# Fused block with a mixture of experts: the first eight expert tiles fixed when the kernel is written, two of them fed by one-hot products

## What is computed

```
x = x + tanh(g_ffn[1]) * ffn(layernorm(x))

logits = gelu(x @ rw1) @ rw2                 # router, E = 8
wgt, idx = top_k(softmax(logits), 2)
for e in range(E):
    Ye = gelu(x @ w1[e] + b1[e]) @ w2[e] + b2[e]
    Ce = gelu(b1[e]) @ w2[e] + b2[e]          # what an expert gives to a token that isn't its own
    for k in range(2):
        mask = idx[..., k] == e
        active = any(mask)
        out += active * wgt[..., k] * where(mask, Ye, Ce)
```

## Time and profile before

| | |
|---|---|
| time, median of 3 runs | 430.28 us (429.59 to 430.42) |
| time of the profiled execution | 430.72 us |
| its span | 428.8 us |
| mean granted TensorE clock in it | 0.898 |
| instructions | 8535 |
| busy: TensorE, VectorE, ScalarE, GpSimd | 319.6, 307.7, 262.0, 166.6 us |
| HBM read, written | 27.43 MB, 6.32 MB |

### The profile page before, as it was taken

One profiled execution on the slowest core, in us unless ns is written; L12 is line 12 of the kernel. 1 busy time (PEld: TensorE's weight loads), 2 busy tenths in 40 slices (PEclk: granted clock), 3 DMA queues, 4 the chain that ended last, 5 costly groups with the idle time before them and its releaser, 6 DMA issues.

```text
span 428.8 us, 8535 instructions
## 1 busy us (share of the span) xinstructions
PE 319.6 (75%) x2638; PEld 216.0 (50%) x2639; DVE 307.7 (72%) x739; ACT 262.0 (61%) x528; POOL 166.6 (39%) x231
## 2 busy tenths in 40 slices
PE   0065988869999968777582511578999999999981
PEld 0054337536477635354341210365777777777760
DVE  3998988863764666759676689466788788888870
ACT  1745656623576476848687598033677777777770
POOL 3041301531284260623671659200355444444422
PEclk9997799989999998979788565678999999999997
DMA  8954000140076073411313535834477777777532
GB/s 265 389 144 136 2 0 2 53 142 2 0 165 233 2 208 72 141 50 51 99 50 99 159 92 147 315 130 171 149 247 248 246 245 245 236 248 233 157 36 24
DMA packets 28097, 60.43 MB, mean 141 GB/s; under 512 B 4401, under 2 KB 19010, under 8 KB 24866
## 3 DMA queue, kind: packets, MB, share of 16 engines
q1 hardware_dynamic: 21186, 52.64, 35.6%
q0 software_dynamic: 4416, 6.13, 8.9%
q10 hardware_dynamic: 2464, 1.27, 1.2%
HBM read 27.43 MB, written 6.32 MB: 79 GB/s over the span
## 4 chain that ended last, share of the span: by engine, by line
DVE 36%; PE 32%; issue 11%; ACT 11%; DMA 4%; POOL 3%; ACTq 1%; DVEq 0%; POOLq 0%
PE bank L1202 6%; PE bank L1544 4%; PE bank L1562 4%; ACT arena L1063 4%; DVE MX L1902 4%; DVE arena L2080 2%; PE bank L1547 2%; PE bank L1163 2%; DVE X L1748 2%; ACT arena L1070 2%; DVE arena L2164 2%; DVE arena L2159 2%; PE bank L1565 2%; DVE stats L1626 2%; ACT arena L945 2%
## 5 line engine op out<-in xcount | busy, mean ns | idle before, releaser
L1063 ACT ACTIVATE arena<-arena,B1D 128x128 f32<-128x128 f32 x184 | 57.6, 392 | 14.3 <-DVE arena L2159 13.7
L1562 PE MATMUL bank<-arena 128*128 x184 | 62.3, 385 | 1.2 <-DVE arena L2164 1.2
L2159 DVE TENSOR_REDUCE arena<-bank 128x256 f32<-128x512 f32 x92 | 57.4, 683 | 4.6 <-PE bank L1547 4.6
L663 POOL TENSOR_TENSOR arena<-STG,arena 128x256 f16<-128x256 f32 x56 | 37.1, 695 | 42.4 <-ACT arena L835 42.4
L663 POOL TENSOR_TENSOR W<-STG,W 128x256 f16<-128x256 f32 x64 | 41.4, 683 | 28.3 <-ACT W L835 28.3
L1565 PE MATMUL bank<-arena 128*128 x184 | 50.7, 276 | 0.0
L734 POOL DMA_INDIRECT out_dram<-arena,SI x23 | 37.3, 1621 | 31.0 <-DMA out_dram<-arena,SI 23.7
L721 POOL DMA_INDIRECT arena<-token_rows,GI x23 | 22.8, 991 | 66.5 <-ACT WS L1057 51.3
L2164 DVE SCALAR_TENSOR_TENSOR arena<-arena 128x512 f16<-128x512 f32 x46 | 29.8, 689 | 24.8 <-ACT arena L1070 24.8
L1544 PE MATMUL bank<-arena 128*128 128x256 f16 x256 | 46.4, 281 | 1.5 <-DVE arena L2127 1.1
L1547 PE MATMUL bank<-arena 128*128 128x128 f16 x256 | 45.4, 225 | 0.0
(11 more groups left out here) (266 smaller groups left out, 708.5 us busy)
## 6 DMA issues: line engine op xcount, KB each, us to landing
STG<-in_l_w_dram SPq DMA_DIRECT2D x32, 512.0 KB, 3.6
arena<-W SPq DMA_DIRECT2D x16, 1024.0 KB, 5.0
STG<-W SPq DMA_DIRECT2D x7, 1024.0 KB
arena<-in_l_w_dram SPq DMA_DIRECT2D x2, 1280.0 KB, 12.2
X<-in_x_dram SPq DMA_DIRECT2D x2, 512.0 KB, 6.1
W<-in_ctx_t_dram ACTq DMA_DIRECT2D x2, 512.0 KB, 11.2
W<-in_ctx_dram SPq DMA_DIRECT2D x1, 1024.0 KB, 17.6
k_parts<-W SPq DMA_DIRECT2D x2, 512.0 KB, 3.3
```

Source lines behind the costliest of these rows:

```text
L663: ins = nc.gpsimd.tensor_tensor(l, src, h, ALU.subtract)
L1063: ins = nc.scalar.activation(x, x, ACT.Gelu, bias=B1D[:, e, c:c + 1], scale=1.0 / (X_SCALE * W_SCALE))
L1562: nc.tensor.matmul(bank[6 + q][:, :], GDL[:, q, 0, c * P:(c + 1) * P], W2[:, e, c].rearrange("p s d -> p (s d)"), start=(c == 0), stop=Fal ...
L2159: v.tensor_reduce(half, o, AX.X, ALU.add).then_inc(s_dadd, 1)
```

## The change

**First eight tiles.** Each expert's first 128 tokens are tile 0 to 7, in the order STATIC = 4, 5, 6, 7, 0, 1, 2, 3, which is known when the kernel is written. They need no EID, no copy of the weights (TensorE reads W1 directly), and no registers. The 15 other tiles take the experts' further tokens. A slot is now the rank within the expert plus ENDT, or plus `place` where the rank is below 128 (early, DIFF).

**Tiles 0 and 1** get their transposed rows as products of the token rows in SBUF (DHL) with one-hot matrices OH (128x1024 each) that come from the ranks (RANK1): 32 products of 128x128 for each tile. Their rows are still gathered, for the row weights alone.

**Slot map and gather.** The products for the slot map (slot_tokens) stand behind tile 0's up product, GI and SI behind tile 0's reductions. GpSimd gathers tiles 2, 3, 0, 1, 4 in this order. Rows and outputs have three buffers. All 23 tiles are written out, without loops.

**Idle shares** move behind tiles 6 to 14 on TensorE: transposes of coefficients at tiles 6 and 7, all 128 products of the idle outputs at 8, the fold at 10, the shares at 11 to 14. ScalarE writes them out (coefficients_out, group_outputs_out, idle_outputs_out, shares_out) over X. SP stores the base X ahead of the tiles (store_base). GpSimd adds the shares, 1 MB, to the output with one direct adding DMA (add_shares) between the adds of tiles 15 and 16.

**Weight blocks.** ScalarE splits blocks 28 to 31 at tiles 3, 4, 5 and 5. GpSimd subtracts for blocks 25 and 26 behind the first five gathers and for 27 to 31 behind the adds of tiles 0 to 4. VectorE's two subtractions fall away. SP's first copy of tile weights (tile 8) waits for all 32 blocks.

The diff, cut to its core:

```diff
@@ constants
+        ONE_HOT = 2
+        STATIC = [*range(E // 2, E), *range(E // 2)]
...
+        SHARES_AFTER = 15
+        def added(j):
+            return 16 * (j + 1 + (j > SHARES_AFTER))
@@ SP
+            def store_base(h):
+                sp.wait_ge(s_dhs, HT * (h + 1))
+                sp.dma_start(out[h * HT * P:(h + 1) * HT * P, :].rearrange("(t p) d -> p t d", p=P),
+                             X[:, h * HT:(h + 1) * HT, :]).then_inc(s_out, 16)
...
             sp.wait_ge(s_eid, 1)
-            sp.wait_ge(s_wlo, W1_BLOCKS)
-            sp.wait_ge(s_rows, 16 * 3)
...
+            sp.wait_ge(s_gi, 2)
+            sp.wait_ge(s_xt_ps, ONE_HOT)
+            sp.wait_ge(s_ws, ONE_HOT)
+            sp.wait_ge(s_wlo, BLOCKS)
+            for j in range(E, TILES):
+                load_tile_weights(j)
@@ GpSimd
+            def add_shares(n):
+                pool.wait_ge(s_share, T)
+                pool.wait_ge(s_sc, 16 * n)
+                pool.dma_start(out[0:N, :].rearrange("(t p) d -> p t d", p=P), X[:, :, :],
+                               accum_op=ALU.add).then_inc(s_sc, 16)
...
-            for j in range(4):
+            for j in (2, 3, 0, 1, 4):
                 gather_rows(j)
+            for i in D_BLOCKS[4:6]:
+                weights_low(i)
...
             for j in range(TILES):
-                if j + 4 < TILES:
-                    gather_rows(j + 4)
+                if j + 5 < TILES:
+                    gather_rows(j + 5)
                 add_to_out(j)
+                if j == SHARES_AFTER:
+                    add_shares(j + 1)
+                if j < BLOCKS - D_BLOCKS[6]:
+                    weights_low(D_BLOCKS[6] + j)
@@ ScalarE
+            def shares_out(t):
+                act.wait_ge(s_base, t // 2 + 1)
+                act.wait_ge(s_out, 32)
+                for i in range(2):
+                    nc.scalar.activation(X[:, t + i], bank[1][:, i * D:(i + 1) * D], ACT.Copy,
+                                         scale=tg[:, 3:4]).then_inc(s_share, 1)
+            for j in range(TILES):
...
+                tile_gelu(j)
...
+                if j >= 3:
+                    low_out(j - 1)
+                if j in (3, 4, 5):
+                    weights_split(D_BLOCKS[4 + j])
+                if j == 5:
+                    weights_split(D_BLOCKS[10])
...
+                if j in (12, 13, 14, 15):
+                    shares_out(2 * (j - 12))
@@ TensorE
+            def one_hot_rows(j):
+                pe.wait_ge(s_oh, j + 1)
+                for k in range(KC):
+                    for s in range(2):
+                        for t in range(T):
+                            mm = nc.tensor.matmul(bank[j][:, (2 * k + s) * P:(2 * k + s + 1) * P],
+                                                  DHL[:, t, s, k * P:(k + 1) * P], OH[:, j, t],
+                                                  start=t == 0, stop=t == T - 1)
+                mm.then_inc(s_xt_ps, 1)
...
+            for j in range(ONE_HOT):
+                one_hot_rows(j)
+            for j in range(TILES):
...
+                tile_up(j, e)
+                if j == 0:
+                    slot_tokens()
+                if ONE_HOT <= j + 1 < TILES:
+                    transpose_tile(j + 1)
+                if j:
+                    tile_down(j - 1, e_before)
...
+                if j == 8:
+                    idle_outputs()
+                if j == 10:
+                    fold_groups()
+                if j in (11, 12, 13, 14):
+                    idle_shares(2 * (j - 11))
@@ VectorE
+            step(v.scalar_tensor_tensor(out=RANK1[:, :, :], in0=rank[:, :, ones_hot], scalar=1.0,
+                                        in1=MSB[:, :, ones_hot], op0=ALU.add, op1=ALU.mult))
+            for j in range(ONE_HOT):
+                v.tensor_tensor(OH[:, j], iota_1[:, :].unsqueeze(1).broadcast_to([P, T, P]),
+                                RANK1[:, :, j:j + 1].broadcast_to([P, T, P]), ALU.is_equal).then_inc(s_oh, 1)
...
+            for j in range(TILES):
+                add_halves(j)
+                if j == 0:
+                    slots_out()
...
+                if j == 1:
+                    tile_experts()
+                    coefficients()
```

More of the change, by code:

```diff
@@ L418, in flamingo @@
         s_base = sem("idle_share_product")
[L419 to L420 removed]
+        s_oh = sem("first_tiles_one_hots_ready")
+        s_xrs = sem("first_tiles_rows_landed")
+        s_xr = [sem(f"tile_rows_landed{i}") for i in range(3)]
+        s_share = sem("idle_shares_in_sbuf")
         s_w1s = [sem(f"tile_weights_landed{i}") for i in range(3)]
@@ L1067, in tile_gelu @@
                     act.wait_ge(s_dg, 2 * j + hb + 1)
-                    if not first:
+                    if j >= 2:
                         act.wait_ge(s_dd, j - 1)
@@ L1452, in _ @@
             pe.wait_ge(s_dconst, 7)
-            for t in range(T):
-                nc.tensor.matmul(bank[5][:, 0:E], ones_b[:, :], MSB[:, t], start=t == 0, stop=t == T - 1)
-            rank = bank[4][:, 0:T * E]
+            rank = bank[7][:, 0:T * E]
             nc.tensor.matmul(rank, before_b[:, :], MSB[:, :, :].rearrange("p t e -> p (t e)"),
@@ L2115, in _, with slots_out @@
-            here()
-            for i in D_BLOCKS[-2:]:
-                _, hi, lo = weight_block(i)
-                dve.wait_ge(s_whi, i + 1)
-                v.tensor_tensor(lo, STG[:, i % 4].rearrange("p (c d) -> p c d", d=D), hi,
-                                ALU.subtract).then_inc(s_wlate, 1)
-            def rows_t(j, q, first=False):
+            one_hot_rows_out(1)
+            def slots_out():
+                dve.wait_ge(s_inv, 1)
+                slot_token1 = bank[6][:, T * E:T * E + TILES]
+                v.tensor_scalar(GI[:, :], slot_token1, -1.0, 0.0, ALU.add, ALU.max).then_inc(s_gi, 1)
+                step(v.tensor_scalar(SIZ, slot_token1, 0.0, spare1[:, 0:1], ALU.is_equal, ALU.mult))
+                v.scalar_tensor_tensor(out=SI[:, :], in0=slot_token1, scalar=-1.0, in1=SIZ,
+                                       op0=ALU.add, op1=ALU.add).then_inc(s_gi, 1)
@@ new lines, in coefficients @@
+            def coefficients():
+                chosen = DTOPF[:, :, :].unsqueeze(3).broadcast_to([P, T, 2, E])
+                mark(v.tensor_tensor(SLOTM[:, :, :, :], M01[:, :, :, :], chosen, ALU.mult))
+                step(v.tensor_tensor(CF[:, :, :, :], ACTV[:, :, :].unsqueeze(1).broadcast_to([P, T, 2, E]), chosen, ALU.mult))
+                step(v.tensor_tensor(IDLE[:, :, :, :], CF[:, :, :, :], SLOTM[:, :, :, :], ALU.subtract))
+                for r in range(2):
+                    mark(v.tensor_tensor(COEF[:, :, r * E:(r + 1) * E], IDLE[:, :, 0], IDLE[:, :, 1], ALU.add))
+                v.tensor_tensor(COEF[:, :, 2 * E:3 * E], CF[:, :, 0], CF[:, :, 1], ALU.add).then_inc(s_coef, 1)
+                here()
@@ L2143, in add_idle_shares, with add_halves @@
-            def add_idle_shares():
-                for t in range(T):
-                    dve.wait_ge(s_base, t // 2 + 1)
-                    v.scalar_tensor_tensor(out=X[:, t], in0=bank[7 if t % 4 < 2 else 1][:, t % 2 * D:(t % 2 + 1) * D],
-                                           scalar=tg[:, 3:4], in1=X[:, t], op0=ALU.mult,
-                                           op1=ALU.add).then_inc(s_base_used, 1)
-            def add_halves(j, q, first=False):
-                if not first:
+            def add_halves(j):
+                q = j % 2
+                if j >= 2:
@@ L2165, in split_hidden, with tile_out @@
                                        op0=ALU.mult, op1=ALU.subtract).then_inc(s_dgl, 1)
-            def tile_out(j, q):
+            def tile_out(j):
                 dve.wait_ge(s_ysa, j + 1)
-                v.scalar_tensor_tensor(out=YS[:, q], in0=bank[6 + q][:, 0:D], scalar=WS[:, q:q + 1], in1=YS[:, q],
-                                       op0=ALU.mult, op1=ALU.add).then_inc(s_ys, 1)
-            for j in range(HEAD):
-                add_halves(j, j % 2, first=j < 2)
-                rows_t(j + 1, (j + 1) % 2, first=j == 0)
+                v.scalar_tensor_tensor(out=YS[j % 3], in0=bank[6 + j % 2][:, 0:D], scalar=WS[:, j % 3:j % 3 + 1],
+                                       in1=YS[j % 3], op0=ALU.mult, op1=ALU.add).then_inc(s_ys, 1)
```

483 lines of the change are left out of this document (238 added, 245 removed).

## The result

The change makes the kernel **slower**: 448.45 us median of 4 runs (444.57 to 451.12) against 429.93 for the kernel before in the same session (427.49 to 430.42), a ratio of 1.044 with a 95% interval of 1.035 to 1.052. Forecast were 428.8 us and a range up to 438. A ratio is worked out from the single executions, so it isn't exactly the quotient of two medians.

The account below looks back on a forecast made before the run. Bound changes by stage: routing, then TensorE in the tiles, then GpSimd's chain of adds. Start -25.5 us, +17.5 given back up to tile 16, transfer 11.6 and the last adds give span 427.3, time 428.8 us; range 420 to 438.

Parts of the forecast that it names:

- the likeliest case: Whole kernel: the forecast itself, with D between 8 and 15, chance 0.40; time 428.8 us, span 427.3.
- The start: -25.5 us: Ahead of the tiles: tile 0 no longer waits for a gather, so tile 2's reductions start at 277.0, not 302.5.
- The ports ... I take 0.2: Tiles beside GpSimd's moved subtractions: port waits with VectorE, 0 to 6.9 us possible, 0.2 us taken.
- Sum 5.0: Early tiles: ScalarE's splits of blocks 28 to 31 behind its write-outs cost 5.0 us.
- 2.8: Tile 8: its first weight copy by SP waits for block 31 and comes 2.8 us late.
- Sum 8.4, nothing hides it: TensorE's additions between tiles: idle outputs 3.9, fold 0.5, shares 4.0; 8.4 us, all of it paid.
- D: Chain of adds: the shares' 1 MB transfer between the adds of tiles 15 and 16, taken as 11.6 us.
- The first rival: Shares' transfer and weight copies share the DMA engines: D 17 to 18, time about 434.5 us; chance 0.26.
- The cheap case: Shares' transfer is cheap, D of 5, so the tiles set the end: time 420.4 us; chance 0.22.
- The adds ahead of the transfer: Tile 15's add starts 6.4 us into tile 16 and has landed 5.0 us later, at 382.6.
- The tail: Behind the transfer: six more adds at 4.6 us to the last one's start, then 5.5 us to the end.
- signs of being wrong: TensorE not full between tiles 9 and 16, adds waiting for VectorE, tile 2 after 282, tile 8 waiting much over 3 us.

Follow-up runs that it names:

- c4: Changed kernel with experts and weight copies early, shares ahead of down products and one tile sooner, one split per tile, GpSimd subtractions one place sooner: 429.47 us, ratio 0.9992.

## Why the prediction was wrong

The start and the end of the forecast were right in mechanism and nearly in size; the likeliest case failed by the tiles between (15.2 of 22 us) and by the adds and the transfer behind them (7.0). Point by point, span 427.3 forecast against 449.3:

- **"The start: -25.5 us"**: right up to tile 1 (tile 0's reductions at 264.77 for 264.2, tile 1's split ended at 274.78 for 274.6, the gather list at 267.17 for 267, L2196 3.65 us for 3). Tile 2's came 4.9 us late: 281.90 for 277.0.
- **"The ports ... I take 0.2"**: this is the step behind those 4.9 us. It counted the subtractions beside the tiles' splits and excused them by ScalarE; it didn't look at the coefficients' operations, which wait for nobody and stand right beside the blocks that had been moved there. The Trainium skill (SBUF — State Buffer, the section on the two sides of the memory) was quoted there and set aside; its rule for operations with two inputs in SBUF fits L2210 and L2258, while L2080 has only one input matrix. The trace agrees that VectorE can wait, and is worse than the one operation, 0.69 us, that the bound took per wait: L2210 lost to eight subtractions in a row, 5.5 us.
- **"Sum 5.0" for the splits and "2.8" for the first copies**: tiles 2 to 8 were forecast with 6 x 5.48 + 1.1 + 5.0 + 2.8 + 0.2 = 42.0 us and took 41.97. That the sum fits so closely is in part luck: one split's wait beside subtractions, 2.6 us (3.88 for 1.29), is in it where 0.2 was set, so the other terms were less; and the wait for the weights was 3.79 us for 2.8, at tile 8's start, which shows partly behind this stretch.
- **"Sum 8.4, nothing hides it"** for TensorE's additions: this is **the step that failed most**. It priced the products' own time and took the order on TensorE as free of waits. Tiles 8 to 12 took 29.3 us for 27.3 (the first two microseconds and more at 1.2 GHz, behind the wait for weights), tiles 12 to 16 took 33.3 for 24.9. The round trip from TensorE to ScalarE and back, three times, and the lower clock cost 8.4 us more than the products: TensorE was idle 4.3 us between 353.2 and 386.4 (0 in the run with the shares ahead), and the other 4.1 it was busy, at clocks down to 0.79. The shares ahead of the down product took both away. With tile 2's 4.9, tile 16 came 15.2 us late, 386.42 for 371.2.
- **"D ... 11.6"**: 13.8 measured, above the bound of 13.1 by the scaled add, at which the forecast's own text set the turn to slower. Alone it is 11.2 to the end of the span, about 10.5 by the chain's measure, so the term from the rate of a short add was near for a transfer without company. The first rival (the shares share the engines) came true by its own mark, D over 13.1, at about half its size: some 3 us more in company, not 6. The cheap case (D of 5) is refuted by the 11.2, and so is the estimate of 4.4 us by the Trainium skill (DMA: Bandwidth & Descriptors, the anatomy of one DMA). The row that the cheap case leaned on, a plain 512 KB store of 2.9 us, doesn't hold still either: in the change's page the same two stores have a median of 5.0.
- **The adds ahead of the transfer** were taken at 5.0 us to landing. Those of tiles 14 and 15 were 6.3 and 7.1 apart from the next start, beside weight copies, and the transfer started 4.8 us later behind tile 16 than forecast. No run isolates why.
- **The tail** was right: six intervals of 4.64 for 4.6, and 5.0 for 5.5 to the end.

The pieces add up: 4.9 at tile 2, 0 to tile 8, 2.0 to tile 12, 8.3 to tile 16, 4.8 at the adds ahead, 2.2 in D, -0.3 in the tail: 21.9 of 22.0 us. Of the signs of being wrong, TensorE not full between tiles 9 and 16 came, tile 8's wait (3.79 us) was somewhat over its 3, and tile 2, at 281.90, just missed its 282. What stays open is whether the waits alone lowered the clock in tiles 12 to 16; the edit removed both together, and no run held the clock and kept the wait.

That the kernel before is no slower than the fully repaired version (c4), whose tile 2 starts 28 us sooner (274.24 for 302.49), has two reasons. Up to tile 14, 14.8 us of the lead go to what now stands between the tiles, so 13.4 are left. The rest goes in the chain of adds: the kernel before stores base and shares together in plain stores ahead of its first add, and its chain holds nothing but the tiles, while in c4 the transfer takes 13.3 us of it. That c4 would gain these without the transfer is argued from the trace; in the change itself the transfer left out gave 12.0.

## What to carry to other kernels

When work moves from an empty stretch into a full one, its price is not its duration: look for each moved step's partner on another engine and ask who waits for whom within one tile, since a short product behind a copy behind another product of the same tile costs a round trip, and here TensorE ran at a lower clock as well. When a serial chain of transfers is nearly as long as the work that feeds it, a transfer put into that chain is paid nearly in full (12.0 of 13.8 us here), and getting the feeding work further ahead doesn't hide it. A stall removed at one engine must be followed to the next queue that gates the same tile, as the one split per tile showed.

## What the runs showed of the hardware

- A two-input operation of VectorE on 120 columns waited through eight subtractions of GpSimd in a row (5.52 us for 0.27), while before the change sixteen one-hots beside twenty subtractions took about as long each as a subtraction, 10.06 us for 16 and 12.89 for 20. Without subtractions beside them the sixteen take 3.65.
- A 1 MB adding transfer from GpSimd's queue took 11.2 us alone, to the end of the span, and up to 13.8 to the next add beside other traffic. A plain 512 KB store had landed in 2.9, and in 5.0 in the change.
- A gather issued 2 us behind that transfer was not there until about when it ended (the next add starts at 416.43). In the change TensorE waited for it until 415.97:

```profile
415.97 0.61 PE L1622 MATMUL bank<-ident_h,arena 128*128 128x128 f16 x4 [6.01 <-DMA arena<-token_rows,GI]
```

  It had been issued at 404.63, 11.3 us earlier; the median gather takes 3.0. The chain of adds hid this stall here.
- TensorE waited some 1.4 us for ScalarE's copy three times, ahead of 359.22, 367.44 and 377.15. The granted clock was 1.00 in the stretch with the first (353.2 to 361.4), 0.92 and 0.87 in those with the next two, and 0.79 in the one behind them. With the waits gone it was 1.00 throughout (353.2 to 386.4).
- The same instructions ahead of the tiles don't take the same time in each execution: tile 0 was written out between 279.1 and 288.5 us in the traces of the change and its edits, and only part of that lies in an edit.
